# TensorE's order in a four-layer conditional residual kernel: the four chunks of the first FFN product in one run between two pairs of attention weighings

## The reference

```python
hidden_i = x @ wi.T
hidden_i += 2 * (x @ common_wi_a.T) @ common_wi_b.T
hidden_i += 2 * (x @ experts_wi_a[e].T) @ experts_wi_b[e].T
hidden_i = relu(hidden_i)             # the first FFN product of L2, 512 wide
```

## Time and profile before

| | us |
|---|---|
| time before, median of 3 runs | 290.99 |
| lowest and highest of the 3 | 288.85, 291.56 |
| the profiled execution's own time | 286.6 |
| its span, first to last instruction | 284.8 |
| mean granted TensorE clock over the span | 0.988 of full speed |

### The profile page before, as it was taken

How to read it: one execution, slowest core, us unless ns; L and a number is a source line. 1 busy time by engine, 2 the same in 40 slices (tenths; PEclk the granted TensorE clock), 3 DMA queues, 4 the chain that set the end, 5 groups by cost and what they waited for, 6 DMA issues and landing times.

```text
span 284.8 us, 14003 instructions
## 1 busy us (share of the span) xinstructions
PE 256.0 (90%) x5498; PEld 188.8 (66%) x5498; DVE 195.6 (69%) x405; ACT 136.0 (48%) x244; POOL 104.2 (37%) x199
## 2 busy tenths in 40 slices
PE   0099999778999999999999999999999998999976
PEld 0065445456877687778777877777777775667845
DVE  2985888759667966797579758985898589342031
ACT  3050644244367345835483549353935393516231
POOL 6051952126321733163316331633164316401250
PEclk9999999987999999999999999999999999999999
DMA  6989823578377706772677267725763775068511
GB/s 163 353 187 218 205 78 98 169 226 245 90 245 236 224 8 197 222 209 75 187 219 218 76 178 221 212 89 169 222 208 101 225 243 163 3 190 243 163 39 39
DMA packets 35954, 48.82 MB, mean 171 GB/s; under 512 B 11201, under 2 KB 16065, under 8 KB 35794
## 3 DMA queue, kind: packets, MB, share of 16 engines
q1 hardware_dynamic: 35922, 48.38, 59.4%
HBM read 44.17 MB, written 4.19 MB: 170 GB/s over the span
## 4 chain that ended last, share of the span: by engine, by line
PE 69%; DVE 7%; DMA 7%; SPq 6%; issue 6%; POOLq 2%; POOL 1%; ACT 1%; DVEq 0%
PE pB L697 8%; PE pB L651 8%; PE pB L652 6%; PE pB L655 6%; PE pB L730 5%; PE pS L625 5%; PE pV L641 4%; PE pA L595 4%; DMA ffn_s<-ffn_w_dram 4%; PE pB L765 3%; PE pA L585 3%; PE pV L609 3%; DVE sc L1042 3%; SPq L264 2%; PE pB L766 2%
## 5 line engine op out<-in xcount | busy, mean ns | idle before, releaser
L358 POOL COPY rw<-e3t_s 128x128 f32 x128 | 38.4, 300 | 52.2 <-issue 42.5
L332 POOL TENSOR_TENSOR sc<-sc,rmax 128x512 f32<-128x512 f32 x32 | 33.6, 1049 | 63.5 <-DVE rmax L1045 63.3
L450 ACT ACTIVATE ex<-sc 128x512 f32<-128x512 f32 x32 | 20.1, 629 | 28.3 <-POOL sc L332 28.3
L730 PE MATMUL pB<-rw,hT 128*32 128x128 f32 x960 | 32.7, 275 | 0.6 <-issue 0.6
L1042 DVE SCALAR_TENSOR_TENSOR sc<-pS,bias 128x512 f32<-128x512 f32 x32 | 21.7, 677 | 11.8 <-PE pS L625 11.7
L730 PEld LDWEIGHTS pB<-rw,hT 128*32 128x32 f32 x960 | 25.0, 109 | 4.6 <-issue 3.9
L697 PE MATMUL pB<-rw,hT 128*32 128x128 f32 x896 | 27.4, 274 | 0.0
L651 PE MATMUL pB<-x_h,ffn_h 128*128 128x512 f32 x50 | 23.3, 466 | 3.4 <-DVE x_h L1096 2.4
L454 ACT ACTIVATE hT<-pB 128x512 f32<-128x512 f32 x28 | 16.7, 598 | 18.6 <-PE pB L655 18.6
L625 PE MATMUL pS<-kb,qs 32*32 32x128 f32 x1024 | 21.8, 278 | 4.0 <-DVE sc L1042 3.3
L697 PEld LDWEIGHTS pB<-rw,hT 128*32 128x32 f32 x896 | 23.7, 110 | 1.5 <-issue 0.8
(11 more groups left out here) (178 smaller groups left out, 492.0 us busy)
## 6 DMA issues: line engine op xcount, KB each, us to landing
rw<-w_d SPq DMA_DIRECT2D x128, 256.0 KB, 3.0
rw<-fc2t_dram SPq DMA_DIRECT2D x4, 768.0 KB, 13.2
xT<-xt_dram SPq DMA_DIRECT2D x8, 256.0 KB, 2.8
xN<-xn_dram SPq DMA_DIRECT2D x8, 256.0 KB, 2.7
w_d<-rw SPq DMA_DIRECT2D x4, 512.0 KB, 3.2
out_dram<-o_s SPq DMA_DIRECT2D x7, 256.0 KB, 2.8
e3t_s<-e3t_dram SPq DMA_DIRECT2D x1, 1024.0 KB, 11.8
ffn_s<-ffn_w_dram SPq DMA_DIRECT2D x1, 896.0 KB, 10.1
```

What stands on the lines that cost most here:

```text
L332: pool.tensor_tensor(sc[:, g % 2, :, :], sc[:, g % 2, :, :], rmax[:, g % 2, :].unsqueeze(2).to_broadcast([P, H, S]), ALU.subtract).then_in ...
L358: pool.tensor_copy(rw[:, r, :, SHARED:D], e3t_s[:, bass.ds(e, 1), :, :].rearrange("p o c n -> p (o c) n"))\
L730: last = mm(ps[S * q:S * q + S, P * g:P * g + P], hT[:, c, tok], rw[:, Q4 * g + q, c, :], start=(c == 0), stop=(c == FC - 1))
```

## The change

The four chunks of the first FFN product now come in one run, with weigh 0 and 1 in front and weigh 2 and 3 behind. In step 1, chunk 0 stays where it was (behind scores 0), and the run is chunks 1 to 3. No instruction is added or removed, and the order of no other engine is touched.

```diff
@@ -838,17 +838,11 @@
                     final(last, 3)
                 scores(n, 3)
                 weigh(n, 0)
-                if last is not None:
-                    hidden(n - 1, 0)
-                    hidden_expert(n - 1, 0)
                 weigh(n, 1)
-                hidden(n - 1, 1)
-                hidden_expert(n - 1, 1)
-                hidden(n - 1, 2)
-                hidden_expert(n - 1, 2)
+                for c in range(1 if last is None else 0, FC):
+                    hidden(n - 1, c)
+                    hidden_expert(n - 1, c)
                 weigh(n, 2)
-                hidden(n - 1, 3)
-                hidden_expert(n - 1, 3)
                 weigh(n, 3)
                 out2(n - 1, 0)
                 if not next_block:
```

## The result

| | median, us | lowest to highest | runs |
|---|---|---|---|
| changed kernel | 286.22 | 283.36 to 290.93 | 14 |
| kernel before, same comparison | 288.77 | 286.25 to 291.56 | 14 |

The ratio of the changed kernel to the kernel before is 0.989, 95% interval 0.985 to 0.993: about 1.1% faster. The profiled execution took 285.52 us, with a span of 283.7. The level of before itself was 2.2 us lower over 14 runs (288.77) than over the three that were shown (290.99).

A forecast was written before the change was run, and what follows sets the result against it. TensorE's queue of matmuls was taken as the bound. Fewer shape changes (-0.29 in step 1, -0.58 in step 2) and steps 3 to 7 with added waits (-1.25) gave -2.1, called 2.0: 290.99 to 289.0 us, range 286.6 to 291.8.

The forecast's parts named there:

- The bound: From weigh 0 to scores 1 of the next step, looped steps are bound by PE alone; TensorE is 90% busy.
- The shape change: Around runs of big matmuls between weighings: each pair removed saves 0.29 us, one in step 1, two in steps 2 to 7.
- the other end for weigh 2: Weigh 2 directly ahead of weigh 3: at 0.40 instead of 0.31, seven steps give 0.6 us less in all.
- the sign of 0.31: In the profile after, weigh 2 to weigh 3 was to take 0.31 us; 0.40 would show the forecast wrong.
- The wait: Weigh 1 waits for turn 1 in steps 3 to 7, 0.33 us each; none in step 2, no change in step 1.
- The sum: Step 1 -0.29, step 2 -0.58, steps 3 to 7 -1.25 us: in all -2.1, called 2.0.
- The steps after: Work behind the moved chunks (relus, exps 3, normalise 0, turn 3, loads, copies) stays covered and costs nothing.
- the tail comes forward as a whole: In step 7 the loads the tail waits for start behind out2 0, so the whole tail moves earlier.
- Rival A: Weigh 1 finds turn 1 done in steps 3 to 7, so the full 3.8 us is gained: 287.2 us; chance 0.12.
- the offset of 0.59 us: Turn 1 ends 0.59 us behind weigh 0's start in steps 1 and 3 to 7, making weigh 1 wait.
- Rival B: TensorE's clock halves in the added wait of steps 3 to 7: +5.2 us, 296.2 us; chance 0.06.
- the level: The saving of 2.0 us is taken off the median of the shown runs, 290.99 us, giving 289.0 us.

The follow-up runs named there:

- the four profiles: Profiles of the changed kernel without further edit, from its first comparison and three repeats; medians 286.22, 285.90, 286.43 and 286.24 us.
- the three later ones: Later comparison rounds in which the unedited kernel before ran beside the experiments; its medians there were 287.50, 287.62 and 287.59 us.
- the four comparisons: The changed kernel, without further edit, measured four times against the kernel before; ratios 0.989, 0.987, 0.9975 and 0.996.
- the changed kernel's third profile: The changed kernel measured a third time, no edit, 12 runs; median 286.43 us, ratio 0.9975 to the kernel before.
- its fourth: The changed kernel measured a fourth time, no edit, 12 runs; median 286.24 us, ratio 0.996 to the kernel before.
- the second profile of before: The kernel before, unchanged, run as a control against itself, 12 runs; median 287.22 us, ratio 1.000.
- its second profile: The changed kernel measured once more, no edit, 6 runs; median 285.90 us, ratio 0.987 to the kernel before.

## Why the prediction was right or wrong

- **The bound.** Right. PE's continuous stretch from weigh 0 on gave its saving one for one in the looped steps: 0.15 us from weigh 0 to out2, 0.14 to 0.15 in the period.
- **The shape change**, 0.29 a pair. Mis-sized: 0.20. Entry 0.11 and exit 0.09 are confirmed in both directions, by removing a pair (0.21) and adding one (0.19). The third part, "a weighing takes 0.40 when 128x128 weights follow, but 0.31 when the 128x32 weights of out2 follow, 0.09 less", was booked as part of the change of shape. It does not come back where out2 follows: two weighings and out2 take 0.71 side by side as apart. Where big matmuls follow, 0.10 comes back (0.70 instead of 0.80, in step 2 and with chunk 0 ahead of scores 3). The prediction had named 0.40 as the other end for weigh 2. The sum came out at that end, though not where it was placed: weigh 3 starts 0.28 us behind weigh 2, so the sign of 0.31 was met, and the time is lost between weigh 3 and out2, 0.42 us where it was 0.31.
- **The wait**, 0.33. The placing was right: weigh 1 starts 0.65 behind weigh 0, 0.64 was taken from step 1. It came five times in addition in the first profile, as said. That step 2 has none is due to a gap of PE without a visible cause ahead of weigh 0, 0.56 us in the first profile of before. The prediction took it for fixed; without it step 2 waits too, as above.
- **The sum.** The terms gave 2.1, called 2.0; the steps gave 1.55. A looped step was to save 0.25 and saved 0.15, and that is most of the difference.
- **The steps after.** Right: relu 0, relu 1, exps 3, normalise and turn 3 stayed covered. One cover was not seen: in step 1 out2 3 waits for its loads in two of the four profiles (below). That the tail comes forward as a whole is not shown. There the out2 3 of the last block waits for a load of its matrices in all six profiles of the two kernels: 0.43 and 0.94 us before, 0.60, 2.21, 0.45 and 2.03 in the changed kernel. From out2 0 of step 7 to that out2 3 it takes 21.8 and 22.3 us before, and 21.9, 23.5, 21.8 and 23.3 after. So up to 1.8 us come and go here, more than the edit is worth, and whether an earlier PE has a part in it is open.
- **Rival A** is out: the offset of 0.59 us held. **Rival B** is out: in the stretch from 110 to 240 us the clock was granted in full in the two profiles of before and in three of the changed kernel that were read for it. The row of its first profile (the clock is the third number from the end):

```profile
110.00:240.00 130.00, 127.70 (x3128) 100.22 (x3120) 102.56 (x203) 74.65 (x135) 49.80 (x97) 1.00 0.62 182
```

- **The step that failed** is the level: "the same difference off the median gives 290.99 - 2.0 = 289.0 us". The median of three runs, spread over 2.7 us, was too high: the 14 runs of before in this comparison have 288.77, and the 81 in the three later ones 287.5 to 287.62. The prediction had seen that its profiled execution lay 4.4 us below that median, and widened its range by only 0.6 us downwards, from 287.2 to 286.6. With 288.77 the same 2.0 us give 286.8, 0.6 from the measured 286.22 and inside the range. With the 1.55 us of the steps it would be 287.2, inside too; the last 1.0 us is near the standard error of 0.75 that a difference of two times 14 runs has. So the second error, the pair of shape changes at 0.29 instead of 0.20, made the saving too large and by luck brought the forecast nearer. The difference itself was forecast as 0.7%; the four comparisons together say 0.6%, and the first alone, 1.1%, was by chance the larger side. That the forecast's 0.7% and these 0.6% agree is partly luck, since the terms were 2.1 us and the steps 1.55.

## What to carry to other kernels

A change between small-tile and full matmuls cost TensorE about 0.2 us in and out here, so matmuls of one shape are worth grouping where nothing is waited for. Before bringing two dependent stages together, read how far the second one's input lags: here it ate the whole gain of one half, and putting the independent work ahead of an existing wait was worth three times the grouping in the period (0.44 against 0.15 us). When runs scatter by 2%, compare the period of a loop step in the profile, and take the base level from many runs.

## What the runs showed that was not expected

**The clock and the start of the pipeline.** In the first profile of before the clock fell to half (1.2 GHz) just at weigh 1 of step 1. In the changed kernel's first profile it did not fall there:

```profile
67.57 0.47 PE L641 MATMUL pV<-vb,pt 128*32 128x36 f32 x32 [0.18 <-DVE pt L1045]
...
77.56 1.08 PE L697 MATMUL pB<-rw,hT 128*32 128x128 f32 x32 [0.66 <-DMA rw<-w_d]
```

The waits just ahead of it were the same in both, 0.94 and 1.24 us for DVE. But in the changed kernel the clock had already been at half around the start of step 1, up to 6 us ahead of weigh 1. The stretches of the two profiles, first before, then the changed kernel (the clock is the third number from the end):

```profile
56.00:59.00 3.00, 3.00 (x48) 2.44 (x40) 1.86 (x4) 0.95 (x2) 0.00 (x0) 0.50 0.73 241
66.50:69.00 2.50, 2.50 (x25) 1.96 (x17) 2.40 (x6) 1.54 (x3) 1.92 (x5) 0.50 0.82 233
```

```profile
57.50:61.00 3.50, 3.50 (x49) 2.79 (x42) 1.87 (x4) 1.65 (x4) 0.00 (x0) 0.53 0.75 217
66.00:70.00 4.00, 3.50 (x105) 2.80 (x106) 3.86 (x8) 1.86 (x3) 3.32 (x8) 1.00 0.81 232
```

So before had two such spells here and the changed kernel one. It goes with the execution and not with the kernel: the changed kernel's third profile has only the early spell, its fourth and the second profile of before only the late one, and its second profile has both. What decides it was not found.

The wait of 0.66 us is for the matrices that out2 3 of step 1 needs. In the fourth profile it was 1.13 us, although the clock had fallen at weigh 1 there; in the second and third there was none. An earlier PE in step 1 can thus be worth nothing when these loads come late.

**The scatter follows the granted clock.** Over 81 executions of the kernel before beside these experiments, those with a mean clock of 0.993 or 0.994 took 286.0 us on average (16 executions), those with 0.987 or 0.988 287.5 (29), those with 0.980 to 0.982 288.5 (24), and the ten below that 291.7; the two at 0.999 took 286.7. In the profiles of the two kernels 0.994 goes with one spell at half clock, 0.988 with two and 0.982 with three, at the start of the pipeline and in the tail. By the averages one spell more is 1.0 to 1.5 us more.

**Two weighings side by side** take 0.70 us whatever follows, one alone 0.31 or 0.40 by what follows, and half a one 0.27. Behind the second one out2 starts 0.42 us later, behind one alone 0.31. What holds it back was not taken apart.
